# Routed rows padded to 128 per expert instead of 256: an expert for each half of a dispatched step, 18 steps instead of 21

## The reference

```python
normed = (xt - mu) * rsqrt(var + LN_EPS) * ln_gamma + ln_beta     # 2048 tokens x 128
probs = softmax(normed @ router_w.T)                              # 8 experts
top_v, top_i = top_k(probs, 2)
gates = softmax(top_v)
comb = sum(one_hot(top_i, E) * gates[..., None], axis=1)
for e in range(E):                                                # gate_up 768x128, down 128x384
    y = silu(gate) * up @ down_w[e].T      # gate, up = split(normed @ gate_up_w[e].T)
    out = out + comb[:, e, None] * y
out = out + _swiglu(normed, shared_gate_up_w, shared_down_w)      # shared expert, width 128
```

## Time and profile before

| what | value |
|---|---|
| median of three runs | 321.99 us (320.24 to 324.29) |
| the profiled execution's own time | 319.61 us |
| its span (first to last instruction of the program) | 317.8 us |
| mean granted TensorE clock | 0.94 of full |
| mean DMA rate | 88 GB/s |

### The profile page before, as it was taken

One profiled execution on the slowest core, in us unless ns is written; L12 is line 12 of the kernel. 1 busy time (PEld: TensorE's weight loads), 2 busy tenths in 40 slices (PEclk: granted clock), 3 DMA queues, 4 the chain that ended last, 5 costly groups with the idle time before them and its releaser, 6 DMA issues.

```text
span 317.8 us, 7526 instructions
## 1 busy us (share of the span) xinstructions
PE 268.3 (84%) x2406; PEld 201.9 (64%) x2406; DVE 236.4 (74%) x711; ACT 204.4 (64%) x469; POOL 158.9 (50%) x206
## 2 busy tenths in 40 slices
PE   7878986997999797999988853878899999999950
PEld 4553442555677464676766732368799999999940
DVE  3586198857977666788999967998576767677796
ACT  2964799796577588976855543535657575756560
POOL 2624297024622546643024777770047878787531
PEclk9999999899999999999999655879999999999995
DMA  7890003001269999970000011113122223111064
GB/s 211 233 383 10 1 2 132 0 3 19 117 188 185 178 181 180 190 105 0 2 1 24 30 45 40 53 49 88 37 71 68 78 67 87 51 32 33 8 226 132
DMA packets 34612, 28.12 MB, mean 88 GB/s; under 512 B 3072, under 2 KB 32389, under 8 KB 33936
## 3 DMA queue, kind: packets, MB, share of 16 engines
q1 hardware_dynamic: 32192, 23.77, 33.8%
q0 software_dynamic: 2240, 3.72, 3.6%
q10 hardware_dynamic: 144, 0.15, 0.2%
HBM read 14.15 MB, written 14.40 MB: 90 GB/s over the span
## 4 chain that ended last, share of the span: by engine, by line
PE 52%; DVE 30%; ACT 8%; issue 6%; DMA 2%; SPq 1%; POOL 1%; DVEq 0%
PE bank L1195 47%; DVE region_k L912 2%; DVE region_x L1152 2%; DVE top L911 2%; DMA wr<-in 2%; PE bank L1492 1%; DVE bn_raw L870 1%; DVE nm L1001 1%; DVE region_k L1003 1%; DVE x L1141 1%; DVE x L1142 1%; ACT x_hat L540 1%; DVE x L902 1%; PE bank L1419 1%; DVE region_k L969 1%
## 5 line engine op out<-in xcount | busy, mean ns | idle before, releaser
L1177 DVE TENSOR_TENSOR region_k<-region_x,region_k 128x768 f16<-128x768 f32 (+1 forms) x33 | 30.6, 926 | 21.6 <-ACT region_k L714 21.6
L1195 PE MATMUL bank<-w_high,region_k 128*128 (+1 forms) x380 | 37.8, 221 | 6.4 <-DVE x L1171 3.3
L1195 PE MATMUL bank<-w_scaled,w_high 128*128 128x256 f16 x252 | 42.5, 273 | 0.1
L846 POOL DMA_INDIRECT expert_rows<-region_k,slot_dest x22 | 27.1, 1232 | 26.5 <-DVE region_k L1164 19.2
L714 ACT ACTIVATE region_k<-region_x 128x768 f16<-128x768 f32 (+1 forms) x33 | 26.8, 813 | 15.8 <-DVE region_x L1152 13.7
L820 POOL DMA_INDIRECT dispatched_rows<-region_t,slot x28 | 28.8, 1028 | 16.1 <-issue 8.3
L1195 PEld LDWEIGHTS bank<-w_high,region_k 128*128 128x128 f16 x380 | 30.9, 99 | 7.7 <-issue 7.3
L1195 PE MATMUL bank<-w_scaled,w_low 128*128 128x256 f16 x126 | 34.3, 273 | 0.0
L1195 PE MATMUL bank<-w_low,region_k 128*128 (+1 forms) x190 | 34.0, 221 | 0.0
L1152 DVE SCALAR_TENSOR_TENSOR region_x<-bank,region_w 128x768 f32<-128x768 f32 (+1 forms) x33 | 30.4, 920 | 3.2 <-ACT region_w L719 2.2
L1195 PE MATMUL bank<-filler 128*128 128x512 f16 x94 | 26.9, 407 | 3.9 <-DVE region_k L912 2.4
(11 more groups left out here) (242 smaller groups left out, 736.1 us busy)
## 6 DMA issues: line engine op xcount, KB each, us to landing
dispatched_rows<-pad_rows SPq DMA_DIRECT2D x8, 1048.0 KB, 18.8
w_scaled<-in SPq DMA_DIRECT2D x5, 1024.0 KB, 8.0
w_scaled<-dispatched_rows SPq DMA_DIRECT2D x21, 131.0 KB, 2.3
region_q<-expert_rows SPq DMA_DIRECT2D x3, 512.0 KB, 5.0
x<-in SPq DMA_DIRECT2D x4, 256.0 KB, 4.4
region_w<-in SPq DMA_DIRECT2D x2, 512.0 KB, 7.0
out<-x SPq DMA_DIRECT2D x3, 256.0 KB, 2.3
w_scaled<-in SPq DMA_DIRECT2D x1, 704.0 KB, 4.1
```

The lines of the kernel that those rows point to most:

```text
L846: pool.indirect_dma_start(ytok, bass.IndirectOffsetOnAxis(dst[:, n, h:h + 1].bitcast(U32), 0), yv[n % 4][:, h * D:(h + 1) * D], None, boun ...
L1177: dve.tensor_tensor(hsplit[:, v, k:2 * k], hid[:, v, 0:k], hsplit[:, v, 0:k], ALU.subtract).then_inc(hidden_low, 1)
L1195: return pe.matmul(o, l, r, start=start, stop=stop)
```

## The change

An expert's rows are rounded up to 128. A step still takes 256 rows, but its two halves of 128 may belong to different experts, so each half has a row address, a load and an expert number of its own. There are at most `HALVES` = (3584 + 8 x 127) // 128 = 35 halves, 18 steps. Tables of 24 and 32 entries become one of 40 (`TTAB`), and the packed word now holds the eight halves of four steps. In `gate_up` each triple of 256 columns becomes two triples of 128 columns, each with the weights of its half's expert. In `down` the number of matmuls stays, but the second half takes its weights from its own expert. The diff, cut to its core:

```diff
-TILES = (2 * NS * P + E * (TP - 1)) // TP
+HALVES = (2 * NS * P + E * (P - 1)) // P
+TILES = -(-HALVES // 2)
 ROUNDS = -(-TILES // 4)
-TTAB = 4 * ROUNDS + 8
+TTAB = 8 * ROUNDS
...
-                row = rows[n] if n < AHEAD else eng.value_load(trow_i[0:1, n:n + 1], min_val=0, max_val=E * REG)
-                eng.dma_start(xd[:, n % 4, :, :], disp[ds(row, TP), :].rearrange("(h p) w -> p h w", p=P)).then_inc(rows_loaded[n % 4], 16)
+                for i in (2 * n, 2 * n + 1):
+                    row = rows[i] if i < 2 * AHEAD else eng.value_load(trow_i[0:1, i:i + 1], min_val=0, max_val=E * REG)
+                    eng.dma_start(xd[:, n % 4, i % 2, :], disp[ds(row, P), :]).then_inc(rows_loaded[n % 4], 16)
...
-                dve.scalar_tensor_tensor(dst[:, n, :], xd[:, n % 4, :, D + 1], te[:, n:n + 1], xd[:, n % 4, :, D],
-                                         ALU.is_equal, ALU.add).then_inc(dest_ready, 1)
+                for h in range(2):
+                    last = dve.scalar_tensor_tensor(dst[:, n, h:h + 1], xd[:, n % 4, h, D + 1:D + 2], te[:, 2 * n + h:2 * n + h + 1],
+                                                    xd[:, n % 4, h, D:D + 1], ALU.is_equal, ALU.add)
+                last.then_inc(dest_ready, 1)
...
                 if kind == "rows":
-                    w = [[v[:, ds(expert, 1), i * P:(i + 1) * P].rearrange("p e n -> p (e n)") for v in gu_w] for i in range(NF)]
                     pe.wait_ge(rows_turned_out, n + 1)
-                    xa, xb = xdt[:, s % 2, 0:TP], xdt[:, s % 2, TP:2 * TP]
+                    parts = [([[v[:, ds(expert[h], 1), i * P:(i + 1) * P].rearrange("p e n -> p (e n)") for v in gu_w] for i in range(NF)],
+                              [xdt[:, s % 2, k * TP + h * P:k * TP + (h + 1) * P] for k in range(2)]) for h in range(2)]
...
-                for i in range(len(w)):
-                    o = psum[:, gate_up_bank(s) * 512 + i * m:gate_up_bank(s) * 512 + (i + 1) * m]
-                    mm(o, w[i][0], xa, True, False)
-                    mm(o, w[i][0], xb, False, False)
-                    last = mm(o, w[i][1], xa, False, True)
-                    if i == (FC if len(w) == NF else 0):
+                for i in range(count):
+                    for h, (w, (xa, xb)) in enumerate(parts):
+                        c = gate_up_bank(s) * 512 + i * m + h * P
+                        o = psum[:, c:c + m // len(parts)]
+                        mm(o, w[i][0], xa, True, False)
+                        mm(o, w[i][0], xb, False, False)
+                        last = mm(o, w[i][1], xa, False, True)
+                    if i == (FC if count == NF else 0):
                         last.then_inc(gate_made, 1)
...
-                    w = [[v[:, ds(expert, 1), i * D:(i + 1) * D].rearrange("p e n -> p (e n)") for v in dn_w] for i in range(FC)]
+                    of = [[[v[:, ds(expert[h], 1), i * D:(i + 1) * D].rearrange("p e n -> p (e n)") for v in dn_w] for i in range(FC)]
+                          for h in range(2)]
```

More of the change, by code:

```diff
@@ L504, in _ @@
             eng.wait_ge(tiles, 1)
-            rows = [eng.value_load(trow_i[0:1, n:n + 1], min_val=0, max_val=E * REG) for n in range(AHEAD)]
+            rows = [eng.value_load(trow_i[0:1, n:n + 1], min_val=0, max_val=E * REG) for n in range(2 * AHEAD)]
             eng.wait_ge(w_low_done, CHUNKS)
@@ L1078, in tiles_counted @@
                 link(dve.tensor_copy(cnt[:, :], bank[6][:, 0:E]))
-                link(dve.tensor_scalar(cnti[:, :], cnt[:, :], float(TP - 1), None, ALU.add))
-                link(dve.tensor_scalar(cnti[:, :], cnti[:, :], 8, None, ALU.logical_shift_right))
+                link(dve.tensor_scalar(cnti[:, :], cnt[:, :], float(P - 1), None, ALU.add))
+                link(dve.tensor_scalar(cnti[:, :], cnti[:, :], 7, None, ALU.logical_shift_right))
                 link(dve.tensor_copy(ntil[:, :], cnti[:, :]))
@@ L1088, in tiles_placed @@
                 link(dve.tensor_reduce(tb[:, :], gn[:, :, :], AX.X, ALU.add))
-                link(dve.scalar_tensor_tensor(trow[:, :], tb[:, :], -float(TP), c32[:, C_STP:C_STP + TTAB], ALU.mult, ALU.add))
+                link(dve.scalar_tensor_tensor(trow[:, :], tb[:, :], -float(P), c32[:, C_STP:C_STP + TTAB], ALU.mult, ALU.add))
                 link(dve.scalar_tensor_tensor(trow[:, :], te[:, :], float(REG), trow[:, :], ALU.mult, ALU.add))
@@ L1093, in windows_packed @@
             def windows_packed():
[L1094 to L1098, removed]
+                link(dve.tensor_scalar(tw[:, :, :], te[:, :].rearrange("p (i j) -> p i j", j=8), float(E - 1), None, ALU.min))
                 link(dve.tensor_tensor(tw[:, :, :], tw[:, :, :],
@@ L1485, in turn @@
             def turn(n):
-                pe.wait_ge(rows_loaded[n % 4], n // 4 * 16 + 16)
+                pe.wait_ge(rows_loaded[n % 4], n // 4 * 32 + 32)
                 wait(pe, rows_turned_out, n)
@@ L1531, in down @@
                 if kind == "rows":
-                    w = [[v[:, ds(expert, 1), i * D:(i + 1) * D].rearrange("p e n -> p (e n)") for v in dn_w] for i in range(FC)]
+                    of = [[[v[:, ds(expert[h], 1), i * D:(i + 1) * D].rearrange("p e n -> p (e n)") for v in dn_w] for i in range(FC)]
+                          for h in range(2)]
                 elif kind == "dense":
-                    w = [[v[:, n, i * D:(i + 1) * D] for v in dn_w] for i in range(FC)]
+                    of = [[[v[:, n, i * D:(i + 1) * D] for v in dn_w] for i in range(FC)]] * 2
                 else:
-                    w = [[v[:, W_SD:W_SD + D] for v in (wh, wl)]]
+                    of = [[[v[:, W_SD:W_SD + D] for v in (wh, wl)]]] * T
                 pe.wait_ge(hidden_low, s + 1)
                 wait(pe, rows_ready, s)
-                m = columns(s) // len(w)
-                for h in range(m // P):
+                m = columns(s) // len(of[0])
+                for h, w in enumerate(of):
                     o = bank[7][:, h * D:(h + 1) * D]
@@ L1557, in expert_of @@
                     return None
-                return e[n % 4] if n // 4 == n_window else before[n % 4]
+                now = e if n // 4 == n_window else before
+                return now[2 * (n % 4):2 * (n % 4) + 2]
             n_window = 0
```

15 lines of the change are left out of this document (8 added, 7 removed).

## The result

| | before | after |
|---|---|---|
| median | 322.37 us (4 runs, 320.24 to 324.29) | 350.76 us (4 runs, 346.75 to 352.34) |
| profiled execution | 319.61 us, span 317.8 | 346.75 us, span 344.9 |
| granted clock, mean | 0.94 | 0.94 |
| first turning of a rows step to PE's last matmul | 89.1 us | 117.1 us |

The ratio is 1.084 (95%: 1.072 to 1.097). Between the two profiled executions the kernel is 27 us slower, and all of it lies in the last stretch of PE: +28.0 us there, -0.7 us behind it.

The account below looks back on a forecast made before the run. Before, PE's array bounded a pass at 3.2 us; after, its sequencer's register instructions would, at 5.1 us. Passes +22.8 and start +0.9 gave +23.7 on 319.6, 343.3 us, taken as 344; range 334 to 354.

Parts of the forecast that it names:

- Rival 1: PE's sequencer keeps up with shorter matmuls, so the array's 3.24 us bounds a pass: faster, 312 us; chance 0.06.
- rival 2: Half hidden: register instructions beside short matmuls cost 0.09 to 0.10 us, passes 3.7 to 4.05, about 319 to 325; chance 0.03.
- rival 3: PE's weight loads are not hidden, each matmul waits for its own 0.098 us: 5.7 us a pass, 356 us; chance 0.03.
- rival 4: PE's granted clock falls to 1.2 GHz, 58 matmuls take 6.2 us a pass: 365 us; chance 0.03.
- 0.126 us for each register instruction: PE's sequencer, line 1195: mean start-to-start distance; 39.5 register instructions in a changed pass take 5.0 us.
- the stretch around the turning: Sequencer time for four matmuls and waits without register arithmetic: 0.1 us added per pass, bounds nothing and 0.22 us.
- two entering passes: Passes with `gate_up` of rows and `down` of dense: 27.5 register instructions, 3.6 us each, together +0.8 us.
- full passes, 19 and 16: Passes with rows in both `gate_up` and `down`: 16 at 5.1 instead of 3.2 us, +30.4; three passes fewer, -9.6.
- Start: Before the first rows step: second load issue +0.6 us and larger planning operations on DVE +0.3, together +0.9.
- second load issue: SP issues two loads a step, so the first rows step is ready later: +0.6 us, bounds 0 and 1.0.
- End: After PE's end, dense results and weighted sums in fixed order on DVE, ACT, POOL: 0, bounds -1 and +0.5 us.
- The rule that was weighed: Skill page: a 128-column matmul in a load-matmul stream costs about 81 ns, making a pass at least 4.7 us by the array.

Follow-up runs that it names:

- experiment 3: Kernel before, packed word kept in two registers and addresses made from both, 34 register instructions a pass instead of 20, same matmuls: 349.75 us, ratio 1.092.
- experiment 1: Changed kernel with fixed expert numbers on PE, no register instructions in rows steps: 313.42 us; kernel before with fixed expert numbers: 321.08 us.
- experiment 2: Changed kernel, but both halves of `down` take the first half's expert, six register instructions fewer a pass: 338.46 us, ratio 1.052.
- experiment 4: Changed kernel, dense steps between rows steps: three 350.81 us, one 349.70; ten single-expert steps 326.43; both: three 333.24, one 327.50, three with later DVE sums 333.62.

## Why the prediction was right

**The direction and the mechanism: shown.** Forecast 344.0, in the range 334 to 354; the measured median is 350.76 (346.75 in the profiled execution). The sequencer's register instructions bound a pass. The evidence is experiment 3 (added without the rest: +29 us), 1 (removed: 350.76 to 313.42, -37 us) and 2 (six removed: -12 us). Rival 1 is excluded by the 0.24 us triples, rival 2 by passes of 5.34 us, rival 3 by the distances in the same triples, which are shorter than its loads, rival 4 by the clock of 1.00 in all full passes. The point forecast is 6.8 us off, over a fifth of the loss: 3.5 us of it are errors of the sum, taken apart below; the other 3.3 are scatter, since the profiled execution (346.75 us) is 4.0 below the median of its four and the forecast had allowed 0.7.

**0.126 us for each register instruction: held** as a mean distance, 4.9 us for 39 distances. The hand-over of the matmuls between them is in it.

**The term that was too small: "the stretch around the turning ... I add 0.1 us".** In the pass read above the last register instruction of one pass starts at 256.22 and the first of the next at 256.57. That is 0.35 us where 0.1 + 0.126 was taken, so this pass has 4.9 + 0.35 = 5.3 us, and the median is 5.34, not 5.1. I had taken less than the array's own 0.22 us for the turning, though the sequencer has to hand over four loads and four matmuls and pass a semaphore there. Sixteen times 0.24 us are 3.8 us.

**The whole sum, stretch by stretch** (us, from start to start on PE in the two profiled executions):

| stretch | before | after | difference | predicted |
|---|---|---|---|---|
| up to the first rows turning | 219.20 | 219.04 | -0.2 | +0.9 |
| two entering passes | 8.90 | 11.13 | +2.2 | +0.8 |
| full passes, 19 and 16 | 60.45 | 85.64 | +25.2 | +22.0 |
| two leaving passes | 5.94 | 5.93 | 0.0 | 0 |
| from there to the end | 23.27 | 23.20 | -0.1 | 0 |
| sum | 317.76 | 344.94 | +27.2 | +23.7 |

The full passes were to cost 30.4 + 1.2 - 9.6 = 22.0 us and cost 3.2 more: 5.34 instead of 5.1 in most, a pass with the word read 0.45 us longer than the others instead of 0.4, less what the first (4.56) and the last (4.87, without a turning) save.

**The overlap that was wrong: the entering passes.** The prediction took the larger of two sums, the array's 3.24 and the sequencer's 3.6 us. The second of these passes, whose `gate_up` is of a rows step and whose `down` is of a dense one without register instructions, took 4.62 us: 0.44 for the turning, 3.18 for `gate_up` at the sequencer's pace (225.99 to 229.17), and then 1.00 for the dense `down` at the array's. The two paces add up within a pass. During that `down` the sequencer got ahead (the register instructions of the next `gate_up` start at 229.5 us, ahead of the turning at 230.17), and this came back in the next pass, which is the one of 4.56 us: 0.8 us, as the prediction had it ("under a microsecond"). In size this error, 1.4 us, comes right behind the one above.

**Start: +0.9 predicted, nothing measured.** The +0.6 for a second load issue was the wrong step. SyncE issues it 0.56 us behind the first (216.19, 216.75), but I left out that the loads are half as large: each lands 0.5 us sooner (1.8 instead of 2.3 us). The planning takes DVE 0.29 us longer, as forecast (2.50 and 2.79 us), but SyncE doesn't wait for it: it waits for the dispatched rows until 215.99 us in both kernels and issues the first load at 216.19 in both.

**End: 0 predicted, and 0 measured.** PE's last matmul ends 8.8 instead of 9.5 us before the end, but that is because PE itself ends 0.6 us later behind its last rows `down`. From that `down` it takes 5.5 us to the first load of `expert_rows` in both kernels, and from there 17.8 and 17.7 us to the end.

**The rule that was weighed.** The Trainium skill's page "TensorE: Matmul & The Clock Gate", section "Back-to-back issue gap", would have made a pass of short matmuls at least 4.7 us. With the registers gone it was 3.24 us, 0.056 us a matmul over 684 of them, each with its load. The rule isn't borne out for this stream. It would have given the right sign here for a wrong reason. As an estimate from the page's 81 ns, a triple would take 3 x 0.081 = 0.24 us, the very distance of the `w_low` matmuls in the changed kernel; experiment 1, with the same matmuls and loads, tells the two apart.

**Where I was wrong in the experiments.** All the expectations of gain from dense steps in between (experiment 4) were too high. The price of the register instructions was right in them; what I left out was the way back of the rows, which those dense steps cover, and the waits that end the sequencer's lead. For the single step in between the medians leave it open, since its expected gain of 2.7 us is about the scatter of the runs; the traces show the gain in the passes and its loss at the end, in one execution each.

## What to carry to other kernels

An address from a register costs nothing while the matmuls that use it keep the array busier than the register instructions keep its sequencer; compare the two before matmuls are halved, and count the register instructions in the new stream. Compare piece by piece and not only by the sums of a pass: the entering pass had 3.6 and 3.24 us of them and took 4.62. Here 20 in a pass of 3.2 us were free and 40 bound it at 5.3. To see it in a profile, read distances from start to start on PE, since the busy share stays at 84% either way; and before an order is changed to give the sequencer rest, look at which transfers the moved steps were covering.

## What the runs showed of the hardware that I had not expected

**Small breaks of PE's sequencer.** The timeline of PE's weight loads in the pass of above (start, duration; a group of two, and one, for each triple) shows them:

```profile
252.07 0.11 PEld L1195 LDWEIGHTS bank<-w_scaled,w_high 128*128 x2 [0.30 <-issue]
252.17 0.10 PEld L1195 LDWEIGHTS bank<-w_scaled,w_low 128*128 x1
...
252.41 0.10 PEld L1195 LDWEIGHTS bank<-w_scaled,w_low 128*128 x1
...
252.65 0.10 PEld L1195 LDWEIGHTS bank<-w_scaled,w_low 128*128 x1
...
252.98 0.10 PEld L1195 LDWEIGHTS bank<-w_scaled,w_low 128*128 x1
...
253.69 0.10 PEld L1195 LDWEIGHTS bank<-w_scaled,w_low 128*128 x1
...
253.97 0.10 PEld L1195 LDWEIGHTS bank<-w_scaled,w_low 128*128 x1
```

The idle time of 0.30 us ahead of 252.07 is no break: two REGISTER_ALU and one ISA stand in a row there, ahead of the first triple of the second half. Most `w_low` loads come every 0.24 us, but between 252.65 and 252.98 there are 0.33 us, and between 253.69 and 253.97 there are 0.28, with the same instructions between them. About a quarter of the triples show such a break, two in the same `gate_up` often 1.0 us apart. Without them a triple with its two register instructions would still need 0.24 us, so they are no cure. What makes them was not tried.

**A register instruction's length says little of its cost.** It is recorded with 32 to 60 ns, costs 0.117 us where six were taken out (experiment 2), and 0.126 us in the pass. A triple of three matmuls and two register instructions takes 0.24 us, three matmuls alone 0.17. The three in a row named above start at 251.77, 251.87 and 251.96 and the load behind them at 252.07: 0.10 us each, with no matmul between them.

**Short matmuls with a load each run at the array's pace** for at least 38 us without a gap, at 0.056 us for 128 columns.
